# Quantising three late weight matrices inside feed-forward instead of in setup

## The chip, the cores and the metric

The kernel runs on one core of one Trainium2 chip. The metric is the device time of one execution in microseconds (us); less is better. A core has five engines with their own instruction streams, which wait for each other by semaphores: TensorE (PE, matmuls and transposes into the eight PSUM banks; PEld is its weight load), VectorE (DVE), ScalarE (ACT), GpSimd (POOL) and SyncE (SP), which here issues every DMA. All DMAs stand in SyncE's stream in a fixed order.

## The reference

x is (4, 512, 512): 2048 tokens of width 512. Four residual steps follow one another:

```python
x = x + jnp.tanh(g_xattn[0]) * _L0_xattn_ref(4, 512, 512, L0_xattn_w, L0_xattn_u, _layernorm(x, axis=-1), ctx_2048)
x = x + jnp.tanh(g_ffn[0]) * _L0_ffn_ref(_layernorm(x, axis=-1), L0_ffn_w1, L0_ffn_w2, L0_ffn_w3)
x = x + jnp.tanh(g_xattn[1]) * _L1_xattn_ref(_layernorm(x, axis=-1), ctx_2048, L1_xattn_wq, L1_xattn_bq, L1_xattn_wkv, L1_xattn_bkv, L1_xattn_wp, L1_xattn_bp)
x = x + jnp.tanh(g_ffn[1]) * _L1_ffn_ref(_layernorm(x, axis=-1), L1_ffn_gamma, L1_ffn_W)
```

The first is a decayed running ratio along the sequence ("mixing"), the second a gated feed-forward with sign weights and group-quantised activations, the third 16-head attention, the fourth a quantised linear layer ("output"). Three 512x512 matrices are quantised before use. wq and wp get one scale per output row, absolute maximum over 127, and integers `clip(round(x / s), -127, 127)`. W of the output layer (`wl` in the kernel) gets one scale for all of it: `clip(round(W * w_scale), -1, 1)` with `w_scale = 1 / (mean|W| + 1e-5)`. Keys and values are `cond @ wkv.T + bkv`, and wkv (1024x512) is not quantised.

## The kernel before

Everything is held in SBUF. X holds the 2048 tokens as 16 row tiles of 128. The stages follow one another.

**Setup** (lines 334 to 348 and the opening part of each engine). Small vectors, three rows spread over all partitions (bv_all, bp_all, gam_all), wkv, X, the first context, wq, wp and wl are loaded. wkv is split into a high f16 part (ScalarE, L665) and a low one (VectorE, L1324). Fourteen groups of eight TensorE transposes (L974, T_GROUPS) turn wkv's two parts (groups 0 to 7), wq, wp and wl (8 to 13); ScalarE copies the even groups out of PSUM (L674), VectorE the odd ones (L1336). Ahead of groups 8 to 13 VectorE finds the maxima of wq and wp (L1341, L1342), rounds (L1347) and makes integers (L1349), and does the same for wl with the mean of its absolute values (L1353 to L1358), which ScalarE has summed (L671) and TensorE spread (L980). wp's scales are spread over the partitions by a diagonal matrix (L1362, L982, L676, swp_all). VectorE also takes the statistics of all 16 X tiles (L1328, L1367), GpSimd the deviations (L500, L501). All engines go on to mixing when the last copies are out.

**Mixing** (16 steps s; b is the batch, k one of four blocks of 128 features). GpSimd normalises x four blocks ahead (`normed`, L519) and forms the numerators (L510). TensorE turns the keys and the context (`context_turn`, L1006, `key_turn`) and projects keys (L1034) and values (L1045). ScalarE makes exponentials, signs of a piece of w1, w2, w3 (L745), and the logarithm and exponential that give the inverse (L706, L708). VectorE runs two scans (L1443, L1454) and the ratio of the step before (`ratio`, L1396), adds bv_all to the values (`values`, L1408) and adds to X (L1383). SyncE stores keys and values, loads pieces and turns the signs by DMA (`turn_weights`, L366).

**Feed-forward** (16 row tiles i, each in four quarters j; c = 4i + j numbers the quarters). TensorE runs `up(i, j)`, 16 matmuls with W1T and W2T, and then `down(i-1, j)`, 8 with W3T. W1's matmuls of quarter c wait for `d_done` of quarter c-2. ScalarE runs `silu`, `round_up` (L780) and `high` (L785), VectorE `hidden` (L1509 to L1514) and `scaled` (L1520), GpSimd the low part (L563), and SyncE turns both parts by one DMA per quarter (`turn_h`, L413) and x of the next tile (`turn_x`, L387). Between the quarters VectorE, ScalarE and GpSimd prepare x for tile i+2 (`prep_...`) and attention's queries (`q_...`, from tile 2 on). Tiles 2k and 2k+1 are one call `tiles(k)`; k = 0, 1 and 7 are written out, 2 to 6 are a loop.

Attention and output follow. WQT is first read at tile 4 (`q_project(0)`, L1100), WPT and WLT in the output stage. Nothing plans the order: each engine does what its own code says, in that order.

## Time and profile before

| | us |
|---|---|
| median of three runs | 973.86 (973.63 to 978.19) |
| the profiled execution | 978.03 |
| its span, first to last instruction | 976.3 |
| TensorE busy | 826.5 (85%) |
| VectorE busy | 760.4 (78%) |
| ScalarE busy | 573.4 (59%) |
| GpSimd busy | 484.2 (50%) |

Setup lasts until about 55 us, mixing until about 220, feed-forward until about 585. Times in a timeline count from the first instruction. "[0.77 <-DVE B L1520]" behind a row says that the engine sat idle for 0.77 us before it, and that VectorE's instruction of line 1520 ended the wait. Durations in the working are of the profiled execution, and sums are made against its 978.03.

### The profile page before, as it was taken

The numbers are of one execution on the slowest core, as the hardware profiler recorded it, in microseconds if no ns is written. First come the engines' busy times: TensorE is split into PE (matmuls) and PEld (weight loads), VectorE is DVE, ScalarE is ACT, GpSimd is POOL, SyncE is SP. The second block draws the span as 40 slices with busy tenths as digits, with TensorE's granted clock in tenths as the row PEclk, the third lists the DMA queues.
The fourth block names the chain that finished last, engine by engine and source line by source line (L and its number), as shares of the span: only waits on it lengthen the run. The fifth ranks groups of instructions, "written<-read, shape, count | busy, mean of one in ns | idle before, by whom it ended". The sixth has DMA issues, their size and how long they took to land.

```text
span 976.3 us, 15239 instructions
## 1 busy us (share of the span) xinstructions
PE 826.5 (85%) x4423; PEld 359.1 (37%) x4423; DVE 760.4 (78%) x1505; ACT 573.4 (59%) x965; POOL 484.2 (50%) x560
## 2 busy tenths in 40 slices
PE   1379988778999999999999978799999999974654
PEld 1235444333444444444444433132323232222321
DVE  3958998887899998999999758477777777724884
ACT  2347888753455656556566554466666666665762
POOL 1086556322334444434444343476767666664761
PEclk9559999989999999999999995799999999996885
DMA  8536987652233323232323332312222121000111
GB/s 278 217 101 181 216 231 194 157 151 45 56 64 64 67 56 62 54 64 54 64 54 61 60 84 69 85 56 62 71 61 70 52 78 49 1 1 0 44 64 65
DMA packets 165163, 84.51 MB, mean 87 GB/s; under 512 B 116960, under 2 KB 149872, under 8 KB 165104
## 3 DMA queue, kind: packets, MB, share of 16 engines
q1 hardware_dynamic: 165104, 83.81, 34.1%
q8 instruction: 27, 0.44, 0.2%
q14 instruction: 32, 0.26, 0.1%
HBM read 37.50 MB, written 12.58 MB: 51 GB/s over the span
## 4 chain that ended last, share of the span: by engine, by line
PE 55%; DVE 8%; SPq 4%; issue 4%; ACT 3%; DMA 3%; POOL 0%; ACTq 0%; DVEq 0%
PE bank L1070 21%; PE bank L1082 10%; PE bank L1157 5%; PE bank L1128 5%; PE bank L1147 4%; DMA A<-B 3%; SPq L432 2%; PE bank L1273 2%; PE bank L1176 2%; PE bank L1166 2%; PE bank L1100 1%; SPq L441 1%; DVE X L1730 1%; DVE B L1611 1%; PE bank L1136 1%
## 5 line engine op out<-in xcount | busy, mean ns | idle before, releaser
L1070 PE MATMUL bank<-A,B 128*128 128x512 f16 x1024 | 232.4, 380 | 3.9 <-DVE B L1520 3.9
L1603 DVE TENSOR_REDUCE B<-bank 128x1 f32<-128x512 f32 x256 | 168.1, 683 | 73.4 <-PE bank L1128 73.3
L895 ACT ACTIVATE A<-bank 128x512 f32<-128x512 f32 x256 | 144.1, 593 | 107.0 <-PE bank L1147 103.5
L563 POOL TENSOR_TENSOR B<-B 128x512 f16<-128x512 f32 x64 | 75.5, 1180 | 209.1 <-ACT B L785 154.7
L1070 PEld LDWEIGHTS bank<-A,B 128*128 128x128 f16 x1024 | 100.2, 98 | 126.2 <-DVE B L1520 4.6
L637 POOL TENSOR_TENSOR B<-A 128x512 f32<-128x512 f32 x64 | 79.4, 1270 | 94.4 <-ACT A L895 94.4
L1082 PE MATMUL bank<-A,B 128*128 128x512 f16 x512 | 120.7, 379 | 0.0
L780 ACT ACTIVATE bank<-B 128x512 f32<-128x512 f32 x64 | 38.5, 602 | 124.6 <-DVE B L1514 124.4
L1147 PE MATMUL bank<-A 98*128 98x512 f16 x256 | 94.9, 392 | 19.5 <-ACT A L895 10.9
L1128 PE MATMUL bank<-A 96*128 96x512 f16 x256 | 98.0, 410 | 7.6 <-DMA A<-B 4.2
L637 POOL TENSOR_TENSOR B<-B,A 128x512 f32<-128x512 f32 x64 | 79.1, 1265 | 1.7 <-ACT A L895 1.7
L1157 PE MATMUL bank<-A,B 128*32 128x512 f32 x512 | 70.4, 623 | 1.0 <-ACT A L895 1.0
L1082 PEld LDWEIGHTS bank<-A,B 128*128 128x128 f16 x512 | 49.5, 98 | 54.3 <-DMA B<-B 0.4
L1045 PE MATMUL bank<-B 128*128 128x512 f16 x192 | 48.4, 406 | 16.7 <-DVE B L1408 16.6
L1520 DVE SCALAR_TENSOR_TENSOR B<-bank,gsm 128x512 f32<-128x512 f32 x64 | 44.2, 691 | 17.1 <-ACT bank L780 15.7
L1509 DVE SCALAR_TENSOR_TENSOR bank<-bank,ffs,B 128x512 f32<-128x512 f32 x64 | 48.3, 755 | 9.4 <-PE bank L1070 6.3
L1128 PEld LDWEIGHTS bank<-A 96*128 96x128 f16 x256 | 23.3, 100 | 84.5 <-DVE B L1603 65.3
L519 POOL TENSOR_SCALAR B<-X,mv,rs 128x128 f32<-128x128 f32 x64 | 49.8, 792 | 1.2 <-DVE WLT L1336 1.2
L775 ACT ACTIVATE B<-bank,ffs 128x512 f32<-128x512 f32 x64 | 43.0, 671 | 10.8 <-PE bank L1070 10.4
L1147 PEld LDWEIGHTS bank<-A 98*128 98x128 f16 x256 | 25.1, 99 | 65.8 <-ACT A L895 36.9
L785 ACT CAST B<-B 128x512 f16<-128x512 f32 x64 | 39.5, 618 | 11.3 <-DVE B L1520 11.3
L1034 PE MATMUL bank<-B 128*128 128x512 f16 x192 | 46.0, 391 | 0.0
(231 smaller groups left out, 1484.1 us busy)
## 6 DMA issues: line engine op xcount, KB each, us to landing
B<-in_L_ffn_w_dram SPq DMA_DIRECT2D x48, 256.0 KB, 3.8
A<-k_parts SPq DMA_DIRECT2D x48, 128.0 KB, 2.6
A<-B SPq DMA_DIRECT2D x192, 32.0 KB, 1.9
X<-in_x_dram SPq DMA_DIRECT2D x4, 1024.0 KB, 13.6
B<-in_ctx_dram SPq DMA_DIRECT2D x16, 256.0 KB, 5.2
k_parts<-B SPq DMA_DIRECT2D x16, 256.0 KB, 4.5
...
```

The costliest lines, as they stand in the source:

```text
L519: last_ = nc.gpsimd.tensor_scalar(XN[:, t, cols], X[:, i, cols], mv[:, i:i + 1, 0], rs[:, i:i + 1], ALU.subtract, ALU.mult)
L563: nc.gpsimd.tensor_tensor(HLb[j][:, 1, :], Db[j % 2], HLb[j][:, 0, :], ALU.subtract).then_inc(lo_done, 1)
L637: nc.gpsimd.tensor_tensor(ACC[j], PR[j] if t == 1 else ACC[j], PR[(HG * t + j) % 8], ALU.add).then_inc(acc_done, 1)
L895: nc.scalar.activation(PR[(HG * t + j) % 8], bank[2 + j % 2][:, :], ACT.Exp, scale=SCALE).then_inc(exp_done, 1)
L1045: last_ = mm(bank[7][:, :], cx[:, j, k * P:k * P + P], wt[:, j, D:2 * D], start=(p == 0 and j == 0), stop=(p == 2 and j == DB - 1))
L1070: last = mm(bank[2 * n + q][:, :], XQT[a][:, m, :], wt[:, m % DB, j * 512:j * 512 + 512], start=(m == 0), stop=(m == 2 * DB - 1))
L1082: last = mm(bank[5 + q][:, :], HT[j][:, m, :], W3T[:, DB * j + m % DB, :], start=(j == 0 and m == 0), stop=(j == FC - 1 and m == 2 * DB - 1))
L1128: mm(bank[ROW_BANKS[r % 3]][:, :], QS[0:96, HG * g + j, t * P:t * P + P], KS[0:96, HG * g + j, :], start=True, stop=True).then_inc(row_ps, 1)
L1147: mm(bank[2 + j % 2][:, :], KS[0:98, HG * g + j, t * P:t * P + P], QS[0:98, HG * g + j, :], start=True, stop=True).then_inc(st_ps, 1)
L1157: last_ = mm(bank[6][DH * j:DH * j + DH, :], VB[:, t, (HG * g + j) * DH:(HG * g + j + 1) * DH], PR[(HG * t + j) % 8], start=(t == 0), stop ...
L1509: stt(H, H, C2, SAb[q], ALU.mult, ALU.mult).then_inc(h_done, 1)
L1603: reduce(NMX[g % 2][:, t, j:j + 1], bank[ROW_BANKS[r % 3]][:, :], AX.X, ALU.max, negate=True).then_inc(row_max, 1)
```

## The change

Setup keeps only wkv. It is loaded in two halves (keys' rows, values' rows) with the first quarter of X between them, and turned half by half, in eight groups. The three spread rows are loaded after the first pieces, behind X's second quarter, and `values(0)` waits for them (`wide_in`). The statistics of X's later batches stand in mixing: those of batch 1 before step 0, one tile of batch 2 or 3 at the start of each step from 0 to 7. GpSimd's deviations stand at steps 0, 4 and 8.

wq, wl and wp go through one buffer (wm_raw, wm_ints) in this order, one to each pair of tiles m = 0, 1, 2:
- SyncE loads wq when mixing is over. At tile 2 it turns the integers of wq by four DMAs into WQT and loads wl; at tile 4 it turns those of wl and loads wp; at tile 6 it turns those of wp, writes wp's scales to memory, waits, and loads them spread into swp_all.
- VectorE: `matrix_scale(m)` (maxima) ahead of quarter 2 of tiles 0 and 4, `mean_scale` ahead of quarter 2 of tile 2, `matrix_ints(m)` ahead of quarter 1 of tiles 1, 3 and 5.
- ScalarE: `matrix_round(m)` at quarter 3 of tiles 0, 2 and 4, `matrix_sum` (sum of |wl|) at quarter 1 of tile 2.
- TensorE: the one-column matmul of that sum at tile 2 behind `up` of quarter 2. The loop now has four turns, and `tiles(2)` is written out.

The core of the diff (eight leading spaces taken off each line):

```diff
+T_GROUPS = [(raw, turned, g) for h in range(2) for raw, turned in ((wkv_hi, WKVH), (wkv_lo, WKVL))
+            for g in (2 * h, 2 * h + 1)]
+WKV_HALF = [slice(4 * D * h, 4 * D * h + 4 * D) for h in range(2)]
...
                     (vrows[12:16, :], by_block(bkv[0:D])),
-                    (TG[:, 0:2], on_all(g_xattn, 2)), (TG[:, 2:4], on_all(g_ffn, 2)),
-                    (bv_all[:, :], on_all(bkv[D:2 * D], D)), (bp_all[:, :], on_all(bp, D)),
-                    (gam_all[:, :], on_all(gamma, D))):
+                    (TG[:, 0:2], on_all(g_xattn, 2)), (TG[:, 2:4], on_all(g_ffn, 2))):
         sp.dma_start(to, frm).then_inc(small_in, 16)
-    sp.dma_start(wkv_raw.rearrange("p (k d) -> p k d", d=D), tiled(wkv)).then_inc(wkv_in, 16)
-    sp.dma_start(X[:, 0:TB, :], x_rows[:, 0:TB, :]).then_inc(x_in[0], 16)
+    for h in range(2):
+        sp.dma_start(wkv_raw[:, WKV_HALF[h]].rearrange("p (k d) -> p k d", d=D),
+                     tiled(wkv)[:, 4 * h:4 * h + 4, :]).then_inc(wkv_in[h], 16)
+        if h == 0:
+            sp.dma_start(X[:, 0:TB, :], x_rows[:, 0:TB, :]).then_inc(x_in[0], 16)
...
-    sp.dma_start(wq_raw, tiled(wq)).then_inc(wqp_in, 16)
-    sp.dma_start(wp_raw, tiled(wp)).then_inc(wqp_in, 16)
-    sp.dma_start(wl_raw, tiled(wl)).then_inc(wl_in, 16)
-    for b in range(1, BATCH):
-        sp.dma_start(X[:, TB * b:TB * b + TB, :], x_rows[:, TB * b:TB * b + TB, :]).then_inc(x_in[b], 16)
...
     pieces(0)
+    sp.dma_start(X[:, TB:2 * TB, :], x_rows[:, TB:2 * TB, :]).then_inc(x_in[1], 16)
+    for to, frm in ((bv_all[:, :], on_all(bkv[D:2 * D], D)), (bp_all[:, :], on_all(bp, D)),
+                    (gam_all[:, :], on_all(gamma, D))):
+        sp.dma_start(to, frm).then_inc(wide_in, 16)
+    for b in range(2, BATCH):
+        sp.dma_start(X[:, TB * b:TB * b + TB, :], x_rows[:, TB * b:TB * b + TB, :]).then_inc(x_in[b], 16)
     for n in range(DB, 2 * DB):
         next_context(n)
...
+    def load_matrix(m):
+
+        if m == 0:
+            sp.wait_ge(mixed, DB * BATCH)
+            sp.wait_ge(key_lo, DB * BATCH)
+        else:
+            sp.wait_ge(wm_ready, m)
+        sp.dma_start(wm_raw, tiled((wq, wl, wp)[m])).then_inc(wm_in, 16)
+
+    def turn_matrix(m):
+
+        sp.wait_ge(wm_ready, m + 1)
+        for k in range(DB):
+            sp.dma_start_transpose((WQT, WLT, WPT)[m][:, :, k * P:k * P + P], wm_ints[:, k, :]).then_inc(wm_out, 16)
+
+    def spread_scale():
+
+        sp.dma_start(swp_dram.rearrange("(k p) -> p k", p=P), SWQP[:, 4:8],
+                     allow_slow_non_contiguous=True).then_inc(swp_io, 16)
+        sp.wait_ge(swp_io, 16)
+        sp.dma_start(swp_all[:, :], on_all(swp_dram, D)).then_inc(swp_io, 16)
+
+    load_matrix(0)
     sp.wait_ge(ff_scales, 1)
     for i in range(TOK):
+        if i in (2, 4, 6):
+            turn_matrix(i // 2 - 1)
+        if i in (2, 4):
+            load_matrix(i // 2)
+        if i == 6:
+            spread_scale()
...
     nc.gpsimd.memset(held[:, :], 0.0).then_inc(consts_set, 1)
-    for b in range(BATCH):
+    def deviations(b):
         cols = slice(TB * b, TB * b + TB)
         pool.wait_ge(stats_ready, b + 1)
...
         nc.gpsimd.tensor_tensor(PHL[:, 1, :], PD, PHL[:, 0, :], ALU.subtract).then_inc(xlo, 1)
-    pool.wait_ge(small_out_dve, 7)
-    pool.wait_ge(small_out_act, 7)
+    deviations(0)
...
     numerators(0)
     for s in range(DB * BATCH):
         k = s % DB
+        if k == 0 and s + DB < DB * BATCH:
...
     step = Chain(act, act_step)
-    act.wait_ge(wkv_in, 16)
...
-    act.wait_ge(wl_in, 16)
-    nc.scalar.activation(T32[:, 2:6, :], wl_raw, ACT.Abs, accum_out=PART[:, 3:4]).then_inc(wl_sum, 1)
-    for g in range(0, len(T_GROUPS), 2):
-        act.wait_ge(small_turned, g + 1)
-        nc.scalar.copy(turned_rows(g), bank_rows(g)).then_inc(small_out_act, 1)
-    act.wait_ge(setup_ps, SETUP["swp_ps"])
-    nc.scalar.copy(swp_all[:, :], bank[7][:, :]).then_inc(small_out_act, 1)
+    for h in range(2):
+        act.wait_ge(wkv_in[h], 16)
+        nc.scalar.activation(wkv_hi[:, WKV_HALF[h]], wkv_raw[:, WKV_HALF[h]], ACT.Copy,
+                             scale=WUP).then_inc(wkv_hi_done, 1)
+        if h == 1:
+            for g in range(0, len(T_GROUPS), 2):
+                act.wait_ge(small_turned, g + 1)
+                nc.scalar.copy(turned_rows(g), bank_rows(g)).then_inc(small_out_act, 1)
...
         up_to(act, hT_in[j], i * 16)
         nc.scalar.copy(HLb[j][:, 0, :], Db[j % 2]).then_inc(hi_done, 1)
+    def matrix_round(m):
+
+        act.wait_ge(wm_scale, m + 1)
+        if m == 1:
+            nc.scalar.activation(wm_raw, wm_raw, ACT.Copy, bias=RND, scale=WS).then_inc(wm_round, 1)
+        else:
+            c = 0 if m == 0 else 4
+            for k in range(DB):
+                last_ = nc.scalar.activation(wm_raw[:, k, :], wm_raw[:, k, :], ACT.Copy, bias=RND,
+                                             scale=RWQP[:, c + k:c + k + 1])
+            last_.then_inc(wm_round, 1)
+
+    def matrix_sum():
+
+        act.wait_ge(wm_in, 16 * 2)
+        nc.scalar.activation(QALL[:, 0, :, 0:2 * 512].bitcast(F32), wm_raw, ACT.Abs,
+                             accum_out=PART[:, 3:4]).then_inc(wm_round, 1)
+
     def q_norm(u):
         act.wait_ge(rstd3, u + 1)
             more = not (last and a == 1)
             for j in range(FC):
                 c = FC * i + j
+                if isinstance(k, int) and k == 1 and (a, j) == (0, 1):
+                    matrix_sum()
...
+                if isinstance(k, int) and k == 1 and (a, j) == (0, 2):
+                    pe.wait_ge(wm_round, SUMMED)
+                    mm(bank[7][:, 0:1], ones[:, :], PART[:, 3:4], start=True, stop=True).then_inc(setup_ps, 1)
                 if not (first and a == 0):
                     down(i - 1, j, 1 - a)
...
+    for h in range(2):
+        dve.wait_ge(wkv_hi_done, h + 1)
+        stt(wkv_lo[:, WKV_HALF[h]], wkv_raw[:, WKV_HALF[h]], WUP, wkv_hi[:, WKV_HALF[h]],
+            ALU.mult, ALU.subtract).then_inc(wkv_lo_done, 1)
+
+    def batch_stats(b, t):
         dve.wait_ge(x_in[b], 16)
-        for t in range(TB):
-            last = nc.vector.bn_stats(st[:, TB * b + t, :], X[:, TB * b + t, :])
-        link(last)
-        for t in range(TB):
-            last = nc.vector.bn_aggr(mv[:, TB * b + t, :], st[:, TB * b + t, :])
-        last.then_inc(stats_ready, 1)
-
-    def small_out(g):
+        i = TB * b + t
+        link(nc.vector.bn_stats(st[:, i, :], X[:, i, :]))
+        last = nc.vector.bn_aggr(mv[:, i, :], st[:, i, :])
+        if t == TB - 1:
+            last.then_inc(stats_ready, 1)
+
+    for t in range(TB):
+        batch_stats(0, t)
...
-        for t in range(TB):
-            last = nc.vector.bn_aggr(mv[:, TB * b + t, :], st[:, TB * b + t, :])
-        last.then_inc(stats_ready, 1)
-    small_out(9)
-    small_out(11)
...
+        if s == 0:
+            dve.wait_ge(wide_in, 16 * 3)
...
+    for t in range(TB):
+        batch_stats(1, t)
     for s in range(DB * BATCH):
         k = s % DB
+        if s + 2 * DB < DB * BATCH:
+            batch_stats(s // DB + 2, k)
         if s > 0:
             ratio(s - 1)
...
+    def matrix_scale(m):
+
+        dve.wait_ge(wm_in, 16 * (m + 1))
+        c = 0 if m == 0 else 4
+        link(reduce(ABSM[:, c:c + 4], wm_raw, AX.X, ALU.max, apply_absolute_value=True))
+        link(ts(SWQP[:, c:c + 4], ABSM[:, c:c + 4], 1.0 / 127.0, 1e-8, ALU.mult, ALU.max))
+        recip(RWQP[:, c:c + 4], SWQP[:, c:c + 4]).then_inc(wm_scale, 1)
+
+    def mean_scale():
+
+        dve.wait_ge(setup_ps, SETUP["wl_mean_ps"])
+        link(ts(LSC, bank[7][:, 0:1], 1.0 / (D * D), 1e-5, ALU.mult, ALU.add))
+        recip(WS, LSC).then_inc(wm_scale, 1)
+
+    def matrix_ints(m):
+
+        dve.wait_ge(wm_round, ROUNDED[m])
+        up_to(dve, wm_out, 16 * DB * m)
+        if m != 1:
+            ts(wm_ints, wm_raw, RND, 127.0, ALU.subtract, ALU.min).then_inc(wm_ready, 1)
+        else:
+            link(ts(wm_raw, wm_raw, RND, -1.0, ALU.subtract, ALU.max))
+            ts(wm_ints, wm_raw, 1.0, None, ALU.min).then_inc(wm_ready, 1)
+
     def tiles(k, first, last):
         for a in range(2):
             i = 2 * k + a
             for j in range(FC):
                 c = FC * i + j
+                if isinstance(k, int) and k < 3 and (a, j) == (0, 2):
+                    mean_scale() if k == 1 else matrix_scale(k)
+                if isinstance(k, int) and k < 3 and (a, j) == (1, 1):
+                    matrix_ints(k)
                 hidden(c, j % 2)
```

Where it moves instructions. A row is an instruction of the named line with its tiles, its shape and what it waits for; x4 stands for four alike. B and A are the two large buffers.

VectorE behind wkv's low part, before:

```order
L1336 COPY B<-bank 128x4x256 [waits small_turned] x2
L1341 TENSOR_REDUCE vec<-A 128x4 [waits wqp_in]
L1342 TENSOR_REDUCE vec<-A 128x4
L1343 TENSOR_SCALAR vec<-vec 128x8 [waits dve_step]
L1344 RECIPROCAL vec<-vec 128x8 [waits dve_step]
L1347 TENSOR_SCALAR A<-A,vec 128x512 [waits dve_step]
L1347 TENSOR_SCALAR A<-A,vec 128x512 x3
L1349 TENSOR_SCALAR B<-A 128x2048 [waits dve_step]
```

and now (L1387 is the copy of the turned groups, L1391 what came last in setup, L1405 mixing's first `low_context`):

```order
L1378 BN_STATS st<-X 128x6 [waits x_in0]
L1379 BN_AGGR mv<-st 128x2 [waits dve_step]
L1387 COPY B<-bank 128x4x256 [waits small_turned] x4
L1391 TENSOR_SCALAR ffs<-vec 128x1 [waits vec_act,consts_set,small_out_act]
L1405 TENSOR_TENSOR B<-bank,B 128x512 [waits ctx_vt,ctx_hi,dve_step]
L1405 TENSOR_TENSOR B<-bank,B 128x512 [waits ctx_vt,ctx_hi] x3
L1378 BN_STATS st<-X 128x6 [waits x_in1]
```

The maxima, roundings and integers are gone from between the copies, and the statistics stand ahead of all four copies and again ahead of mixing's first scan.

SyncE at tiles 1 and 2 of feed-forward (`turn_h` is L413 before and L412 now, `turn_x` L387 and L380), before:

```order
L413 DMA_TRANSPOSE B<-B 128x8x128 [waits down_ps,lo_done,hi_done]
L387 DMA_TRANSPOSE B<-B 128x8x128 [waits b_ps,xlo,xhi]
L413 DMA_TRANSPOSE B<-B 128x8x128 [waits down_ps,lo_done,hi_done] x4
L387 DMA_TRANSPOSE B<-B 128x8x128 [waits b_ps,xlo,xhi]
L413 DMA_TRANSPOSE B<-B 128x8x128 [waits down_ps,lo_done,hi_done] x4
```

and now:

```order
L412 DMA_TRANSPOSE B<-B 128x8x128 [waits down_ps,lo_done,hi_done]
L380 DMA_TRANSPOSE B<-B 128x8x128 [waits b_ps,xlo,xhi]
L412 DMA_TRANSPOSE B<-B 128x8x128 [waits down_ps,lo_done,hi_done] x3
L455 DMA_TRANSPOSE WQT<-B 128x4x128 [waits wm_ready]
L455 DMA_TRANSPOSE WQT<-B 128x4x128 x3
L449 DMA B<-in_L_ffn_W_dram 128x4x512 [waits wm_ready]
L412 DMA_TRANSPOSE B<-B 128x8x128 [waits down_ps,lo_done,hi_done]
L380 DMA_TRANSPOSE B<-B 128x8x128 [waits b_ps,xlo,xhi]
L412 DMA_TRANSPOSE B<-B 128x8x128 [waits down_ps,lo_done,hi_done] x4
```

Four transposes to WQT and wl's load stand between tile 1's last `turn_h` and tile 2's first.

ScalarE at tile 2 (`high` of quarter 0, then `prep_hi`, `round_up`, `silu` and `high` of quarter 1), before:

```order
L785 CAST B<-B 128x512 [waits hT_in0,d_done]
L731 CAST B<-B 128x512 [waits xhl,xT_in0]
L780 ACTIVATE bank<-B 128x512 [waits silu_done,t_done]
L775 ACTIVATE B<-bank,ffs 128x512 [waits h_done,a_ps]
L785 CAST B<-B 128x512 [waits hT_in1,d_done]
```

and now (L831 is `matrix_sum`):

```order
L814 CAST B<-B 128x512 [waits hT_in0,d_done]
L831 ACTIVATE B,ffs<-B 128x4x512 [waits wm_in]
L760 CAST B<-B 128x512 [waits xhl,xT_in0]
L809 ACTIVATE bank<-B 128x512 [waits silu_done,t_done]
L804 ACTIVATE B<-bank,ffs 128x512 [waits h_done,a_ps]
L814 CAST B<-B 128x512 [waits hT_in1,d_done]
```

The sum over wl, which waits for its load, has come between `high` of quarter 0 and all of quarter 1.

## Rows read from the trace of the kernel before

**Rows 1.** Busy table, 12 us: span, PE, PEld, DVE, ACT, POOL, granted clock, DMA, GB/s.

```profile
36.00:48.00 12.00, 3.42 (x33) 2.86 (x32) 11.79 (x25) 3.04 (x3) 1.20 (x2) 0.60 0.19 68
```

**Rows 2.** Timeline of VectorE in setup: start, duration, line, tiles, shapes, [idle before, releaser].

```profile
18.23 4.42 DVE L1324 SCALAR_TENSOR_TENSOR A<-A 128x4096 f16<-128x4096 f32 x1 [6.22 <-ACT A L665]
...
26.54 2.27 DVE L1341 TENSOR_REDUCE vec<-A 128x4 f32<-128x2048 f32 x1
...
33.20 1.23 DVE L1349 TENSOR_SCALAR B<-A 128x2048 f16<-128x2048 f32 x1
...
53.40 0.69 DVE L1336 COPY WLT<-bank 128x1024 f16<-128x1024 f16 x1 [0.53 <-PE bank L974]
```

**Rows 3.** Timeline of TensorE in setup.

```profile
18.25 3.40 PE L974 MATMUL bank<-id,A 128*128 128x128 f16 x32 [8.77 <-ACT A L665]
...
55.85 1.09 PE L1006 MATMUL bank<-id,B 128*128 128x128 f32 x8 [0.68 <-ACT swp_all L676]
```

**Rows 4.** Timeline of GpSimd at the end of setup.

```profile
54.36 12.43 POOL L519 TENSOR_SCALAR B<-X,mv,rs 128x128 f32<-128x128 f32 x16 [1.22 <-DVE WLT L1336]
66.75 1.27 POOL L510 TENSOR_TENSOR B<-B 128x512 f32<-128x512 f32 x1
```

**Rows 5.** Timeline of VectorE in mixing's steps 0 and 1.

```profile
65.34 1.23 DVE L1443 TENSOR_TENSOR_SCAN bank<-vec,bank 128x512 f32<-128x512 f32 x1 [2.73 <-ACT bank L699]
...
72.25 0.70 DVE L1396 TENSOR_TENSOR bank<-bank,B 128x512 f32<-128x512 f32 x1 [2.46 <-ACT B L708]
```

**Rows 6.** Waits from 60 to 228: who waits, for whom, us in total, times, longest.

```profile
DVE bank L1396 <- ACT B L708: 8.2, 8, 2.5
```

**Rows 7.** Timeline of TensorE in feed-forward.

```profile
239.32 3.61 PE L1070 MATMUL bank<-A,B 128*128 128x512 f16 x16 [0.77 <-DVE B L1520]
...
286.63 3.62 PE L1070 MATMUL bank<-A,B 128*128 128x512 f16 x16
...
346.90 3.40 PE L1070 MATMUL bank<-A,B 128*128 128x512 f16 x15
```

**Rows 8.** Timeline of VectorE in feed-forward.

```profile
285.25 0.69 DVE L1520 SCALAR_TENSOR_TENSOR B<-bank,gsm 128x512 f32<-128x512 f32 x1
...
344.49 0.69 DVE L1520 SCALAR_TENSOR_TENSOR B<-bank,gsm 128x512 f32<-128x512 f32 x1 [0.67 <-ACT bank L780]
```

**Rows 9.** DMA issues: out<-in, times issued, KB each, median us to landing.

```profile
out_dram<-X SPq DMA_DIRECT2D x8, 512.0 KB, 2.8
A<-in_L_xattn_wkv_dram SPq DMA_DIRECT2D x1, 2048.0 KB, 10.0
...
A<-B SPq DMA_TRANSPOSE x48, 2.5
```

**Rows 10.** Timeline of ScalarE in setup.

```profile
14.58 3.62 ACT L665 ACTIVATE A<-A 128x4096 f16<-128x4096 f32 x1 [12.49 <-DMA A<-in_L_xattn_wkv_dram]
```

**Rows 11.** Timeline of VectorE in feed-forward, statistics of one tile.

```profile
229.39 0.69 DVE L1415 BATCH_NORM_STATS2 st<-X 128x6 f32<-128x512 f32 x1
...
230.12 0.18 DVE L1417 BATCH_NORM_AGGREGATE mv<-st 128x2 f32<-128x6 f32 x1
```

**Rows 12.** Timeline of ScalarE in feed-forward's tiles 0 to 2.

```profile
243.80 0.60 ACT L780 ACTIVATE bank<-B 128x512 f32<-128x512 f32 x1 [3.97 <-DVE B L1514]
...
269.80 0.62 ACT L785 CAST B<-B 128x512 f16<-128x512 f32 x1 [0.15 <-DVE B L1520]
...
273.84 0.60 ACT L780 ACTIVATE bank<-B 128x512 f32<-128x512 f32 x1 [2.91 <-DVE B L1514]
```

**Rows 13.** Timelines of SyncE's queue, and of GpSimd in tile 1.

```profile
212.83 3.84 SPq L366 DMA_TRANSPOSE A<-B  x3
...
265.84 1.16 POOL L563 TENSOR_TENSOR B<-B 128x512 f16<-128x512 f32 x1 [4.78 <-ACT B L785]
```

**Rows 14.** Timeline of TensorE in mixing's last steps.

```profile
193.02 5.30 PE L1045 MATMUL bank<-B 128*128 128x512 f16 x12 [3.64 <-DVE B L1408]
```

**Rows 15.** Busy table, 2 us; columns as in rows 1, clock third from the end.

```profile
194.00:196.00 2.00, 2.00 (x7) 0.62 (x6) 1.49 (x2) 1.52 (x3) 1.15 (x1) 0.50 0.65 174
```

More of the change, by code:

```diff
@@ L843, in _ @@
             tiles(1, False)
-            with act.Fori(2, TOK // 2 - 1) as k:
+            tiles(2, False)
+            with act.Fori(3, TOK // 2 - 1) as k:
                 tiles(k, False)
@@ L1117, in _ @@
             tiles(1, False, False)
-            with pe.Fori(2, TOK // 2 - 1) as k:
+            tiles(2, False, False)
+            with pe.Fori(3, TOK // 2 - 1) as k:
                 tiles(k, False, False)
@@ L1374, in _ @@
[L1374 to L1375 removed]
+            dve.wait_ge(small_out_act, len(T_GROUPS) // 2)
+            dve.wait_ge(consts_set, CONSTS["all"])
             dve.wait_ge(vec_act, 2)
```

122 lines of the change are left out of this document (40 added, 82 removed).

## The prediction

> **What bounds the kernel now.** I read four views in this order: the busy table by stretches, the timelines of the engines through setup, the waits and the timeline of mixing's steps, and the timelines of feed-forward's first tiles. In setup TensorE has next to nothing to do: 3.42 us of the 12 us from 36 on, while VectorE is busy for 11.79 [rows 1]. VectorE is working through the three later matrices, and it hands over the last copy of WLT at 53.4 to 54.1 [rows 2]. Only then do TensorE's context transposes start, at 55.85 [rows 3], and GpSimd's sixteen normalising instructions, at 54.36; these take 12.43 and the numerators behind them end at 68.02 [rows 4]. The weights and scans of step 0 come at 65.34, and the first ratio waits 2.46 for ScalarE's logarithm and starts at 72.25 [rows 5]. In mixing VectorE is nearly full: over 16 steps its ratio waits 8.2 us in all, eight times, 2.5 of it in step 1 [rows 6]. In feed-forward's tile 0 TensorE waits for VectorE (0.77 before the group at 239.32), and after that it never stops [rows 7]. But VectorE is only just ahead. The W1 matmuls of quarter c need VectorE's scaled quarter c-2: that of quarter 13 is done at 285.25 + 0.69 = 285.94 and the matmuls start at 286.63, a lead of 0.69; for quarter 24 it is 344.49 + 0.69 = 345.18 against 346.90, a lead of 1.72 [rows 7, 8]. So work that is put on VectorE there is paid for in full, but for about 1.4 us once.
>
> **Setup: what goes.** Time before is counted against the profiled execution. The path is now: second half of wkv, its high part, VectorE's low part, VectorE's statistics, its four copies, contexts.
> - wkv's 2 MB landed about 10.0 us after issue [rows 9], and ScalarE started on it at 14.58 [rows 10]. The new order puts wkv half, X, wkv half: 3 MB, but without the three broadcast loads ahead of them (0.75 MB), so the second half should land at much the same time. At wkv's 5.0 us per MB X adds 5.0 and the broadcasts drop 3.8, which gives 15.8; but part of X was in flight while wkv landed, so I take 14.7. Bounds 13.5 (all of X was) and 17.7 (the broadcasts had cost only half of that).
> - Half of the 3.62 high part [rows 10] is 1.8: 16.5. Half of the 4.42 low part [rows 2] is 2.2: 18.7. Four linked pairs of statistics at 0.69 + 0.18, overlapping to about 0.84 a pair [rows 11], are 3.4: 22.1.
> - The copies now stand behind the statistics. First two 1.3 (0.69 each [rows 2]); TensorE turns group 5 after the first, then 6 and 7, at 3.40/4 = 0.85 each [rows 3]: 22.8 + 2.6 = 25.4; last copy 0.7: 26.1.
> The contexts start at 26.1 where they started at 55.85: **29.7 earlier**. GpSimd no longer waits for the copies: it needs the statistics (22.1), 1.3 for the deviation, then 12.43 and 1.27 [rows 4], so the numerators are there at 37.2, 30.8 earlier. VectorE puts four more statistics pairs (3.4) and one of step 0 (0.8) in front of the first scan. They shift it from 65.34 - 29.7 + 1.5 to about 37.4, but step 1's ratio waited 2.46 anyway [rows 5], so the first ratio comes 29.4 earlier. I take **-29.4**; bounds -31 (wkv at 13.5) and -26 (at 17.7).
>
> **Mixing: what comes in.** Eight statistics pairs stand ahead of the ratio in steps 0 to 7, 0.84 each. That of step 0 and that of step 1 lie in the waits just named. Six are left: 5.0. The other seven waits of the ratio hold 5.7 in all [rows 6]; I count 3 of it, the half that falls into these steps and the one after, as filled by the new work. **+2**; bounds 0 and +5. The three GpSimd deviation pairs (1.2 each) stand before work that GpSimd does early, at nothing; if that cover were gone they would cost 1.2 three times. In values(0) the wait for the wide rows is free: they land some 20 us before.
>
> **Feed-forward: what comes in.** I follow VectorE's delay D and TensorE's delay, which is D less the lead.
> - Tile 0, quarter 2: absolute maximum of wq, 2.27 [rows 2], and two small instructions, 2.76 with links. TensorE already waits for VectorE here: D = 2.8. ScalarE's four roundings in quarter 3 take about 2.6 and fit into its wait of 3.97 [rows 12].
> - Tile 1, quarter 1: integers of wq, 1.23 [rows 2]: D = 4.0.
> - Tile 2 is the dear one. SyncE gets to WQT's transposes when it has issued those of quarter 7; GpSimd's low part of it ended at 265.84 + 1.16 = 267.0 [rows 13], now 271.0. Then 1.2 for that transpose, four of 1.28 (3.84 for three [rows 13]), so the load of wl is issued at about 277.4 and 1 MB lands some 4.5 later (512 KB took 2.8 [rows 9]), at 282. ScalarE is at its abs-sum after the cast of quarter 8, which ended at 270.4 [rows 12], now 274.4, and stands **7.6 us** with everything behind it: its own sum of 1.91 (half of the 3.62 for 4096 columns, [rows 10]), prep_hi's 0.6, and the rounding of quarter 9. This rounding started at 273.84 [rows 12], would be at 277.8, and is at 284.6: 6.8 later, D = 10.8. TensorE waits for the same sum before the down-projection. Bounds 5.5 (load lands in 3.2) and 9.
> - Quarter 10: two small ones, 0.4. Tile 3, quarter 1: WLT's clamp and integers, twice 1.23: D = 13.7.
> - Tile 4: the same queue for wp. The load lands about 1 us after VectorE asks; with 2.76 for the maximum D = 17.5. ScalarE's roundings again fit. Tile 5: 1.23, D = 18.8.
> - TensorE's delay is 18.8 - 1.4 = **17.4**.
> - Tile 6: SyncE issues four transposes (5.1), writes 512 single words, waits until they have landed and issues the broadcast. The transpose of tile 7's x stands behind. It needs to land some 15 us after quarter 23 and does so after about 1.2 + 5.1 + 4.5 + 0.5 + 1.3 + 2.5 [rows 9] = 15.1. No row shows such a write: it can't take less than nothing, and by its 512 pieces I set it at 4.5, above the 2.8 of [rows 9]; with the h transpose that also stands ahead I count **+1.2**, bounds 0 and +5.
> - **+0.9** for the clock, below. Feed-forward: **+19.5**, bounds +13 and +26.
>
> **The clock.** Before the twelve value matmuls at 193.02 TensorE stood idle for 3.64 and they took 5.30 [rows 14], at a granted clock of 0.50, which is 1.2 GHz [rows 15]; at 2.4 GHz they would take half. The wait in tile 2 is longer, the one in tile 4 about as long. So 2 to 3 us of matmuls run at 1.2 GHz after each. After tile 2 VectorE's 2.5 us of tile 3 cover it; after tile 4 about 0.9 sticks. The Trainium skill (TensorE: Matmul & The Clock Gate, "HAM oscillation") says that every wait that re-throttles the array is paid again in slow matmuls; by that rule alone both would cost, some 2.5 each, and the total would be 4 us higher than mine. The trace agrees on the halved clock; whether it is hidden behind VectorE no row shows.
>
> **Sum**: -29.4 + 2 + 19.5 = -7.9. The profiled execution took 978.03 and would take 970.1; the median of the three runs is 973.86, so the forecast is **966.0**. Attention and the output stage are the same instructions on the same data.
>
> **The rivals.**
> 1. *Feed-forward costs its work alone.* If wl and wp land before they are asked for, the 6.8 shrinks to sum and prep_hi that fit into the wait of 2.91 [rows 12], and the 1 us of tile 4 and the clock's share go: about 9 less, 957. For it: the loads are only 1 MB. Against: SyncE can't issue them before four transposes. Chance 0.17.
> 2. *Both ends are dearer.* The second wkv half lands at 17.7 (+3) and mixing swallows none of the pairs (+3), or both waits drag the clock: 970 to 978, say 974. For it: VectorE is the fullest engine in mixing. Chance 0.23.
> 3. *Slower: the matrices' transposes go one after the other.* If each holds the queue for its own 2.5 us [rows 9] rather than for 1.28 of issue, each matrix takes 10 instead of 5. Then the waits of tiles 2 and 4 are 5 longer each and tile 7's x lands 5 later: 966 + 15 = 981. It decides from the point where one transpose holds the queue over 2.3 us. Against: three issued in 3.84 let ScalarE go on soon after. The Trainium skill (Advanced Engine Details and Errata, X-Bar Transpose) calls them as fast as plain transfers on this chip; no row here sets the two side by side. Chance 0.12.
> 4. *It doesn't take setup off the path*, because something else still holds the contexts until about 55: none of the engines has such work left. Chance 0.03: about 990.
>
> **How the numbers follow.** Forecast 0.45 (960 to 971), and the rivals as given. A measurement tells about 0.5%, 4.9 us, from no change: faster is below 969.0, slower above 978.7. Faster: 0.17, and three quarters of 0.45, and a little of rival 2: 0.54. Slower: 0.12 + 0.03 and the top of rival 2: 0.16. Same: 0.30. Range 955 to 978: it leaves out rivals 3 and 4.
>
> **What would show it.** First context transpose near 26, first ratio near 43, feed-forward's first matmul near 193 (220.64 - 27.4). ScalarE's abs-sum should show a wait of 7 to 8 for a DMA, TensorE one of about 6 before the single-column matmul, and the feed-forward stage should be 19 longer. A stage only 10 longer is rival 1; contexts after 30 or ratios that no longer wait at all are rival 2; waits of over 12 in tile 2 are rival 3.

## The result, and the profile after

The changed kernel takes **978.88 us** (median of 20 runs), the kernel before beside it 976.64 (20 runs): ratio 1.003, 95% interval 1.0021 to 1.0039. Forecast were 966.0, with 955 to 978. So 29 us of setup were won, and feed-forward spent slightly more than that. The profiled execution has a span of 975.0 at a mean granted clock of 0.948. It is the shortest of its 20 (976.90), and that of the kernel before (978.03) lies 1.4 above its median. So the two traces compared below differ by -1.1 where the medians differ by +2.2; these 3.4 us are not explained here.

Setup of the changed kernel, as timelines give it (start, duration, engine, line, tiles, shapes, count, [idle before, releaser]). The first three rows answer [rows 3] and [rows 4], the last answers [rows 5].

```profile
26.31 1.09 PE L1045 MATMUL bank<-id,B 128*128 128x128 f32 x4 [0.83 <-ACT B L705]
...
23.55 12.43 POOL L546 TENSOR_SCALAR B<-X,mv,rs 128x128 f32<-128x128 f32 x16
35.94 1.27 POOL L537 TENSOR_TENSOR B<-B 128x512 f32<-128x512 f32 x1
...
43.15 0.70 DVE L1410 TENSOR_TENSOR bank<-bank,B 128x512 f32<-128x512 f32 x1 [0.48 <-ACT B L737]
```

Contexts at 26.31 instead of 55.85, the first ratio at 43.15 instead of 72.25: 29.1 earlier.

Where it went is read at one landmark per quarter: the start of VectorE's first instruction on a quarter's hidden rows (line 1509 before, 1529 after), in both timelines. Each tile has four. The fourth column is how much of the gain the tile spent.

| tile | quarter 0, before | after minus before | spent in the tile | forecast |
|---|---|---|---|---|
| 0 | 225.39 | -29.20 | 2.3 | 2.8 |
| 1 | 245.27 | -26.88 | 1.0 | 1.2 |
| 2 | 265.69 | -25.85 | 8.4 | 7.2 |
| 3 | 286.87 | -17.48 | 3.5 | 2.5 |
| 4 | 308.47 | -13.99 | 5.0 | 3.8, and 0.9 of clock |
| 5 | 330.36 | -9.00 | 1.0 | 1.3 |
| 6 | 352.59 | -8.01 | 7.2 | 1.2 |
| 7 | 374.48 | -0.81 | 0.2 | 0 |
| 8 to 13 | 396.74 | -0.59 | 0.1 | 0 |
| 14 | 528.98 | -0.52 | 1.5 | 0 |
| 15 | 549.58 | +1.00 | 0 | 0, and 1.4 of lead given back |

Feed-forward spent 30.2 where 19.5 were forecast (1.4 of lead taken off), and mixing nothing where 2 were. Behind the landmark of tile 15 the difference goes from +1.0 to -1.3 at the end of the span. That is attention and the output stage, the same instructions on both sides; over all the runs below this part comes out between -2.3 and +0.7, and nothing here says why.

The landmark is VectorE's. TensorE's groups of 16 matmuls tell the end of the story better:

```profile
349.18 3.62 PE L1109 MATMUL bank<-A,B 128*128 128x512 f16 x16
...
376.09 3.62 PE L1109 MATMUL bank<-A,B 128*128 128x512 f16 x16
...
546.92 3.62 PE L1109 MATMUL bank<-A,B 128*128 128x512 f16 x16
```

Before, these three groups start at 358.15, 375.09 and 545.92. So TensorE is 8.97 early in the middle of tile 6, and from the second quarter of tile 7 on it is 1.00 late. From there to tile 15 it never waits, in either trace, and the 1.00 stays. By TensorE's reckoning the stretch around tile 6 costs 10.0 and not 7.2, and tile 14 costs nothing: the 1.5 there is only VectorE's distance from TensorE that changes.

The dear tiles, in the timelines of ScalarE, VectorE and TensorE:

```profile
253.69 1.91 ACT L831 ACTIVATE B<-B 128x2048 f32<-128x2048 f32 x1 [9.13 <-DMA B<-in_L_ffn_W_dram]
...
255.75 0.59 PE L1157 MATMUL bank<-ffs,ones 128*128 128x1 f32 x2 [7.55 <-ACT B L831]
256.20 3.20 PE L1121 MATMUL bank<-A,B 128*128 128x512 f16 x8
...
307.79 2.29 DVE L1580 TENSOR_REDUCE vec<-B 128x4 f32<-128x2048 f32 x1 [2.66 <-DMA B<-in_L_xattn_wp_dram]
...
368.55 5.08 PE L1109 MATMUL bank<-A,B 128*128 128x512 f16 x16 [8.35 <-DMA B<-B]
```

In tile 2 ScalarE stands 9.13 at the sum of absolute values, and TensorE 7.55 for that sum. In tile 4 VectorE waits 2.66 for the third matrix. At the start of tile 7 TensorE waits 8.35 for a DMA, x's transpose; the kernel before has no such stop. SyncE's queue shows what stood ahead of these DMAs: the first two rows are of tile 2, the others of tile 6.

```profile
242.49 5.20 SPq L455 DMA_TRANSPOSE WQT<-B  x4
247.74 0.58 SPq L449 DMA_DIRECT2D B<-in_L_ffn_W_dram  x1
...
346.74 5.20 SPq L455 DMA_TRANSPOSE WPT<-B  x4
351.98 0.58 SPq L459 DMA_DIRECT2D swp_row<-vec  x1
360.80 0.33 SPq L462 DMA_DIRECT2D swp_all<-swp_row  x1
361.24 3.63 SPq L412 DMA_TRANSPOSE B<-B  x1
364.98 1.25 SPq L380 DMA_TRANSPOSE B<-B  x1
```

The load of the second matrix is issued at 247.74, behind four transposes. The write of the 512 scales is issued at 351.98, and only at 360.80, 8.8 later, can SyncE go on. It issues the broadcast of the scales, then the transpose of hidden rows, whose issue takes 3.63 where 1.23 is usual; x's transpose (line 380) follows at 364.98.

### The profile page after: what moved, and what is told of

The parts are those of the page before. It is cut to its first block, busy times and chain, and to the rows that moved or that the text cites. A ratio compares the mean times of both kernels' runs of the same rounds, so it can differ in the third digit from the quotient of the medians.

```text
span 975.0 us, 15020 instructions
## 1 busy us (share of the span) xinstructions
PE 822.8 (84%) x4373; PEld 354.8 (36%) x4373; DVE 750.3 (77%) x1492; ACT 576.2 (59%) x971; POOL 487.7 (50%) x560
## 4 chain that ended last, share of the span: by engine, by line
PE 43%; DVE 15%; issue 6%; SPq 6%; DMA 5%; ACT 4%; POOL 1%; ACTq 0%; DVEq 0%; POOLq 0%
PE bank L1109 13%; PE bank L1121 6%; PE bank L1203 5%; PE bank L1174 5%; PE bank L1193 4%; DMA A<-B 3%; PE bank L1320 2%; SPq L431 2%; PE bank L1222 2%; PE bank L1212 2%; DVE bank L1529 2%; SPq L455 2%; DVE gsm L1531 1%; DVE B L1534 1%; DVE B L1540 1%
## 5 line engine op out<-in xcount | busy, mean ns | idle before, releaser
L1109 PE MATMUL bank<-A,B 128*128 128x512 f16 x1024 | 236.0, 384 | 19.7 <-DVE B L1540 11.3
L1121 PE MATMUL bank<-A,B 128*128 128x512 f16 x512 | 121.9, 382 | 0.0
L1193 PE MATMUL bank<-A 98*128 98x512 f16 x256 | 93.8, 388 | 20.6 <-ACT A L947 10.9
L1529 DVE SCALAR_TENSOR_TENSOR bank<-bank,ffs,B 128x512 f32<-128x512 f32 x64 | 48.4, 757 | 22.3 <-PE bank L1109 20.2
L1531 DVE TENSOR_REDUCE gsm<-bank 128x8 f32<-128x512 f32 x64 | 44.3, 692 | 2.2
```

Source lines behind the costliest of these rows:

```text
L1109: last = mm(bank[2 * n + q][:, :], XQT[a][:, m, :], wt[:, m % DB, j * 512:j * 512 + 512], start=(m == 0), stop=(m == 2 * DB - 1))
L1121: last = mm(bank[5 + q][:, :], HT[j][:, m, :], W3T[:, DB * j + m % DB, :], start=(j == 0 and m == 0), stop=(j == FC - 1 and m == 2 * DB - 1))
L1193: mm(bank[2 + j % 2][:, :], KS[0:98, HG * g + j, t * P:t * P + P], QS[0:98, HG * g + j, :], start=True, stop=True).then_inc(st_ps, 1)
L1529: stt(H, H, C2, SAb[q], ALU.mult, ALU.mult).then_inc(h_done, 1)
L1531: link(reduce(gsm[:, 0, :], grouped(H), AX.X, ALU.max, apply_absolute_value=True))
```

## The experiments

Each landmark difference below is, as above, against the kernel before, in the profiled execution. Each ratio is against runs of the kernel before on the same chip.

**Setup alone.** Edit: every call of `load_matrix`, `turn_matrix`, `spread_scale`, `matrix_scale`, `mean_scale`, `matrix_round`, `matrix_sum` and `matrix_ints` out, and a constant in their tiles, set by GpSimd ahead of tile 0. The kernel then leaves out the quantising, and its output is not the reference's.

```diff
-                if i in (2, 4, 6):
-                    turn_matrix(i // 2 - 1)
-                if i in (2, 4):
-                    load_matrix(i // 2)
-                if i == 6:
-                    spread_scale()
```

> Left out: all of the three matrices' work in feed-forward (loads, sums, maxima, rounding, integers, the twelve transposes, the scattered write and its broadcast); the tiles that later read them hold a constant instead, so the output is not the reference's. My theory: setup gives its 29 us and mixing keeps them, and everything that was lost was lost in feed-forward. Quarter 0 of tile 0 then stands 29.2 us before that of the kernel before, and the last quarter of tile 15 too: 976.6 - 29.3 = 947 us, between 945 and 950. Rival A: feed-forward of the changed kernel loses time also without the matrices' work (the batches' statistics, the wide rows, a clock that falls): over 955. Rival B: attention gives some of the lead back: feed-forward ends 29 earlier, but the time is over 952.

Measured: 946.17, ratio 0.9694 (0.967 to 0.9718). The landmark is at -29.68 in tile 0, -29.69 in tile 3, -30.58 in tile 8 and -29.68 in tile 15. Setup's gain is whole, mixing and attention take nothing of it, and all that the changed kernel lost is the matrices' work in feed-forward.

**The wait for the scattered write moved to tile 8** (write_apart), and **the loads issued early** (load_early), alone and together (both_moves).

```diff
             def spread_scale():
...
-                sp.wait_ge(swp_io, 16)
-                sp.dma_start(swp_all[:, :], on_all(swp_dram, D)).then_inc(swp_io, 16)
+            def fetch_scale():
+                sp.wait_ge(swp_io, 16)
+                sp.dma_start(swp_all[:, :], on_all(swp_dram, D)).then_inc(swp_io, 16)
...
+                if i == 8:
+                    fetch_scale()
```

```diff
-                if i in (2, 4):
-                    load_matrix(i // 2)
...
                 for j in range(FC):
+                    if i in (1, 3) and j == 2:
+                        load_matrix((i + 1) // 2)
                     turn_h(i, j)
```

> All is computed. The scattered write of the 512 scales is issued at tile 6 as before, but SyncE waits for it and issues the broadcast at tile 8. My theory: the wait for that write (351.98 to 360.80 in the changed kernel) held the transposes of tile 6 and with them tile 7's x; of the 7.2 us that tile 6 costs, 5.5 to 7.2 go: 971.7 to 973.5 us, and no wait of TensorE over 2 us near the start of tile 7. Rival A: the four matrix transposes ahead of it (5.2 us of SyncE) are what held x, and the write came beside: at most 3 us go, 976 us or more, with a wait of 4 us or more left at tile 7. Rival B: the wait at tile 8 only moves the loss there: 978 to 980 us.

> All is computed. The loads of the second and the third matrix are issued ahead of the third quarter's transpose of tiles 1 and 3 (as soon as the buffer is free) and no longer behind the four transposes of tiles 2 and 4, so they land over 15 us earlier. My theory: ScalarE's 9.13 us wait at the sum of absolute values and the 2.7 us wait ahead of the third matrix's maximum go. Tile 2 then costs 2 to 4 us and not 8.4, tile 4 2.8 to 3.5 and not 5.1: together 6 to 8.5 us less, 970.5 to 973 us. Rival A: the cost is the passes themselves, which VectorE and ScalarE execute at whatever time: 977 us or more. Rival B: the earlier loads now hold the transposes of tiles 1 and 3 (a transpose behind a load took 2.29 to 2.85 us to issue, not 1.23), and give back 2 to 3 us: 974 to 976 us.

> All is computed. Both edits of write_apart and load_early. My theory: the waits are at different tiles and the lead of VectorE does not carry from one to the other, so the gains add up: 963.5 to 967.5 us, which is 9 to 13 us faster than the kernel before. Rival A: one of the two waits covered part of the other's cost (while TensorE stands, VectorE catches up and pays for passes that otherwise cost time themselves), so that 3 us or more of the sum is missing: 968 to 971 us.

Measured: 975.8, ratio 0.9997 (0.9982 to 1.0011); 966.93, 0.9904 (0.9877 to 0.993); 963.16, 0.9867 (0.9843 to 0.9892). load_early saved more than expected, 10.9 us at tile 15's landmark: tile 2 now spends nothing (landmark -26.57 to -26.87, a gain of 0.3) instead of 8.4, and tile 4 2.3 instead of 5.0. ScalarE's sum starts without a wait; the load had been issued at 231.54.

```profile
243.75 1.91 ACT L831 ACTIVATE B<-B 128x2048 f32<-128x2048 f32 x1
```

So ScalarE's whole pass is free there; what tiles 0, 3 and 4 still spend (2.3, 3.5 and 2.3) is near the length of VectorE's passes, and for these alone rival A holds. write_apart missed: tile 6 still spends 4.4 of its 7.2, or 6.5 of 10.0 by TensorE. Its SyncE queue and TensorE:

```profile
352.76 0.58 SPq L459 DMA_DIRECT2D swp_row<-vec  x1
353.45 1.24 SPq L412 DMA_TRANSPOSE B<-B  x1
354.80 1.27 SPq L380 DMA_TRANSPOSE B<-B  x1
...
365.56 6.10 PE L1114 MATMUL bank<-A,B 128*128 128x512 f16 x16 [3.80 <-DMA B<-B]
```

x's transpose is issued at 354.80 and not at 364.98, but TensorE gets x only 10.8 later. SyncE's wait was only part of the matter. both_moves adds the gains up. The ratios fell from 1.003 to 0.9997 and 0.9904 by the single edits and to 0.9867 by both, which is 1.6 points either way; at tile 15's landmark it is 14.8 against 10.9 and 2.0, where single profiles of one setup already differ by 1 us at tile 0's.

**The write behind x** (write_after_x, on top of both_moves).

```diff
-                if i == 6:
-                    spread_scale()
                 for j in range(FC):
                     turn_h(i, j)
                     if j == 0 and i < TOK - 1:
                         turn_x(i + 1, (i + 1) % 2)
+                    if i == 6 and j == 0:
+                        spread_scale()
```

> All is computed. both_moves, with the scattered write of the scales issued in tile 6 behind the transpose of tile 7's x and no longer ahead of it. In both_moves and write_apart x was issued in time (354.80) and still landed at 365.6, while the 16 DMA engines were busy and moved 8 to 33 GB/s. My new theory: the write itself keeps the DMA engines for 8 to 10 us and what is issued behind it lands behind it; behind x it only delays hidden rows, which are due a tile later. Tile 6 then costs under 0.7 and not 4.2 us: 958.5 to 960 us. Rival A: the four matrix transposes ahead of x are what delays it: 962.5 us or more, with TensorE's wait of 3 us or more left. Rival B: the delayed transposes of hidden rows hold TensorE's second multiplication: 960 to 963 us, with waits on those rows.

Measured: 955.42, ratio 0.9787 (0.9762 to 0.9813); once more, with five rounds, 954.43, ratio 0.9776 (0.9748 to 0.9803).

> The kernel of write_after_x once more, beside sliced_two_turns on the same chip, to tell the two apart and to set its gain on the kernel before: 955 to 957 us, ratio 0.977 to 0.981.

```profile
334.15 5.21 SPq L455 DMA_TRANSPOSE WPT<-B  x4
339.46 1.24 SPq L412 DMA_TRANSPOSE B<-B  x1
340.81 1.27 SPq L380 DMA_TRANSPOSE B<-B  x1
342.14 0.57 SPq L459 DMA_DIRECT2D swp_row<-vec  x1
...
347.46 3.62 PE L1114 MATMUL bank<-A,B 128*128 128x512 f16 x16
```

The four matrix transposes still stand ahead of x, and TensorE starts tile 7 at 347.46 without a wait; tile 6 spends nothing (-20.59 to -21.14; TensorE stays at -21.56). The four transposes thus cost nothing, and the order of two DMAs is worth some 8 us.

**Queue or engines** (write_on_act, write_on_act_late): the write is issued by ScalarE, on a queue of its own; in the first between tiles 5 and 6, in the second inside tile 6, which is written out for it.

```diff
             tiles(2, False)
+            act.dma_start(swp_dram.rearrange("(k p) -> p k", p=P), SWQP[:, 4:8],
+                          allow_slow_non_contiguous=True).then_inc(swp_io, 16)
```

```diff
+                        if isinstance(k, int) and k == 3 and (a, j) == (0, 1):
+                            act.dma_start(swp_dram.rearrange("(k p) -> p k", p=P), SWQP[:, 4:8],
+                                          allow_slow_non_contiguous=True).then_inc(swp_io, 16)
                         if more and j == 1:
                             x_turned(act, k, a)
                             prep_hi(i + 1)
```

> All is computed. both_moves, with the scattered write issued by ScalarE, on a DMA queue of its own, between tiles 5 and 6; SyncE's queue has only its transposes there. If the order in SyncE's queue is what delays x, the wait of 3.8 us goes: 958.5 to 960.5 us. If the 512 small elements keep the DMA engines themselves, whichever queue they are in, x lands as late as in both_moves: 962 to 964 us. I hold the engines for likelier, 6 to 4.

> All is computed. In write_on_act the write was issued at 330.3, so that it had landed (9.5 us) when tile 7's x was issued at 340.68, and that run does not tell the queue from the engines. Here ScalarE issues it in tile 6, right ahead of its last operation on x, 1 to 3 us before SyncE issues x's transpose (in both_moves SyncE's own queue had the write 2 us ahead of x, and TensorE went on 12.3 us after the write, having waited 4.04). If what waits is only what stands behind the write in the same queue: no wait of TensorE for x, 954 to 957 us. If the 512 small elements keep the DMA engines for everyone: x lands some 12 us after the write's issue, a wait of 3 to 5 us as in both_moves, 960 to 963 us. I now hold the queue for likelier, 6 to 4: in the changed kernel the DMA engines stood at a busy share of 0.44, 0.10, 0.00 and 0.00 in the four stretches of 2 us in which SyncE waited for the write.

Measured: 956.68, ratio 0.9796 (0.9776 to 0.9816), and 957.91, ratio 0.9801 (0.9779 to 0.9824). For x the first can't tell the two apart: it issued the write at 330.3, and its landing 9.5 later was over before x was issued. But SyncE's transposes right behind it tell:

```profile
330.31 0.41 ACTq L895 DMA_DIRECT2D swp_row<-vec  x1
...
332.27 1.23 SPq L412 DMA_TRANSPOSE B<-B  x1
```

This one landed 9.3 after its issue, where 3.0 is the median of the kernel before, and the four matrix transposes behind it 8.3 down to 5.2, where write_after_x has 2.5. They came late although the write was in another queue, and it cost nothing, since none of them was due. The second run shows the same for x:

```profile
337.06 0.40 ACTq L877 DMA_DIRECT2D swp_row<-vec  x1
...
341.66 1.27 SPq L380 DMA_TRANSPOSE B<-B  x1
...
350.70 5.31 PE L1112 MATMUL bank<-A,B 128*128 128x512 f16 x16 [2.24 <-DMA B<-B]
```

Nothing but transposes is in SyncE's queue, and TensorE still waits 2.24 and goes on 9.0 after x's issue and 13.6 after the write's; in both_moves it was 12.3 after the write's. So in both profiled executions a queue of its own did not protect what SyncE issued behind the write, and my 6 to 4 for the queue was the wrong way. How much it helps is open: the second's execution was the longest of five, 962.4 with a median of 957.9, which lies between the two forecasts, so in others x may have waited less. Busy table of the same run (span, PE, PEld, DVE, ACT, POOL, clock, DMA share, GB/s):

```profile
342.00:344.00 2.00, 2.00 (x11) 0.90 (x10) 1.94 (x7) 1.85 (x4) 0.35 (x1) 1.00 2.12 70
344.00:346.00 2.00, 2.00 (x11) 0.94 (x10) 1.86 (x5) 0.23 (x1) 1.77 (x5) 1.00 1.57 13
```

The 16 engines have packets open for all of the time and move 13 GB/s in the second stretch. When the write was alone in the changed kernel, the share was 0.10 and 0.00 from 354 to 358, so it is slow without filling the engines. Whether it is the elements in DRAM or their acknowledgement that takes 9 us, no run tells.

**The second matrix's passes where GpSimd is idle** (ints_quiet, on top of write_after_x).

```diff
-                        if isinstance(k, int) and k < 3 and (a, j) == (1, 1):
+                        if isinstance(k, int) and k in (0, 2) and (a, j) == (1, 1):
                             matrix_ints(k)
                         hidden(c, j % 2)
+                        if isinstance(k, int) and k == 1 and (a, j) == (1, 3):
+                            matrix_ints(k)
```

> All is computed. write_after_x, with the second matrix's two passes on VectorE moved from the start of the second quarter of tile 3 to the inside of its fourth, and what follows for the third matrix one or two quarters later. In the changed kernel these passes took 2.18 and 2.06 us, and GpSimd's subtractions beside them 2.13, while in setup the same passes took 1.23 and GpSimd's 1.15. My theory: the two engines' 128-partition passes hinder each other when they meet; in the fourth quarter GpSimd is idle by then, so the passes take 1.2 to 1.3 us each, and 1.5 to 2.1 us less than write_after_x are seen at tile 3; the time is 1 to 2 us under write_after_x's. Rival: the passes are slower for another reason that holds all through feed-forward (the transfers, the place of the buffer): 2.0 us or more each, and no difference.

Measured: 955.75, ratio 0.9774 (0.975 to 0.9798), not told apart from write_after_x. But the passes did as expected. First the changed kernel, at tile 3 with GpSimd beside them and at tile 1 with VectorE's start just ahead of GpSimd's, then ints_quiet:

```profile
274.52 2.18 DVE L1597 TENSOR_SCALAR B<-B 128x2048 f32<-128x2048 f32 x1
275.58 2.13 POOL L560 TENSOR_TENSOR B<-B 128x512 f16<-128x512 f32 x1
276.74 2.06 DVE L1598 TENSOR_SCALAR B<-B 128x2048 f16<-128x2048 f32 x1
...
223.30 1.20 DVE L1595 TENSOR_SCALAR B<-B 128x2048 f16<-128x2048 f32 x1
223.33 2.17 POOL L591 TENSOR_TENSOR B<-B 128x512 f16<-128x512 f32 x1 [3.14 <-DVE B L1540]
```

```profile
279.44 1.22 DVE L1602 TENSOR_SCALAR B<-B 128x2048 f32<-128x2048 f32 x1
280.69 1.23 DVE L1603 TENSOR_SCALAR B<-B 128x2048 f16<-128x2048 f32 x1
```

From tile 2's third quarter to tile 4's second the landmark loses 1.8 and not 3.3 as in write_after_x; the third matrix's work, which had to move too, then costs 0.6 more (its integers 2.0 and not 1.4). So it is shown that the two engines hinder each other here; the 0.9 that is left is too little for the measurement. The rows say more than that. In the changed kernel the later starter pays: at tile 1 VectorE began 0.03 ahead of GpSimd and took its 1.20, and GpSimd took 2.17 instead of 1.16. At tile 3 GpSimd had begun 0.27 ahead (line 591, 274.25 to 275.62), and VectorE's first pass took 2.18; the subtraction that began inside that pass took 2.13.

**Work in slices** (sliced, sliced_two_turns). All of the matrices' work is cut in blocks of 128 x 512, with three load buffers; one block in a quarter. The core of VectorE's part, with c the quarter counted from tile 0, and the edit that makes sliced_two_turns of sliced, which had one such transpose for each c from 12 to 15 (the mean of the second matrix also comes a quarter earlier, at c = 14):

```diff
+                            if 2 <= c < 6:
+                                matrix_max(0, c - 2)
+                            if 8 <= c < 12:
+                                matrix_ints(0, c - 8)
+                            if 12 <= c < 16:
+                                matrix_max(2, c - 12)
...
+                    if c in (12, 13):
+                        turn_matrix(0, 2 * j)
+                        turn_matrix(0, 2 * j + 1)
```

> All is computed. The matrices are loaded into three buffers of their own, at tiles 0, 1 and 2, and all of their work is cut in blocks of 128 x 512: one block in a quarter of a tile on ScalarE and VectorE (on VectorE between the scaling and the rounded result, where it waits for ScalarE), one transpose in a quarter on SyncE, the scattered write behind the second quarter of tile 6. In the kernel before VectorE is idle for some 39 of 360 us in feed-forward, 0.6 us in a quarter. My theory: passes of 0.3 to 0.9 us in a quarter mostly fit in there, and only what is over 0.6 costs: 2 to 5 us over setup_alone's 946.2, 948 to 951.5 us. Rival A: what is executed on VectorE costs in full however it is cut, since its lead is used up by the next quarter: some 12 to 14 us, 958 to 961 us. Rival B: the finer work adds waits and instructions: 953 to 957 us.

> All is computed. sliced, with the first matrix's four transposes two in each of tile 3's first two quarters (they were one in each of its four), and the mean of the second matrix a quarter earlier. In sliced, TensorE waited 9.2 us ahead of the first projection of queries: it is due at the start of tile 4, and the last transpose was issued only at 285.09, behind the hidden rows of tile 3's last quarter. My theory: that wait goes whole (7.5 us at the landmark of tile 4), and the blocks cost 6 to 8 us over setup_alone's 946.2: 952 to 954.5 us, 1 to 3.5 under write_after_x. Rival: the 9.2 us gave VectorE and ScalarE time for blocks that they now pay for elsewhere: 955 to 958 us, no faster than write_after_x.

Measured: 960.02, ratio 0.9825 (0.9806 to 0.9845), and 952.23, ratio **0.9746 (0.9719 to 0.9773)**. sliced was slow by a wait that I had built in. Its last transpose of WQT stood behind tile 3's last hidden rows:

```profile
285.09 1.27 SPq L458 DMA_TRANSPOSE WQT<-B  x1
...
287.82 1.87 PE L1146 MATMUL bank<-B,WQT 128*128 128x128 f16 x16 [9.19 <-issue]
```

With two transposes in each of two quarters this wait is gone and so are the 7.5 us at the landmark. The fixed version spends 6.5 from tile 0 to tile 6 (-30.88 to -24.36), write_after_x 9.8. What is sliced does not vanish in VectorE's idle time, as I had hoped (rival A was nearer for sliced, but for another reason), but about 3 us less are spent; the three load buffers and other partners on GpSimd came with it, and how much each of them gave was not separated. It is 24.7 us faster than the kernel before and the fastest that does all of the work; beside write_after_x on the same chip it is 2.2 us faster, at overlapping intervals.

## Why the prediction was wrong

- **Tile 6, +1.2: the step that failed.** It priced the scattered write's landing at 4.5, above a plain transfer's 2.8, and that nearest row was far off: it took 8.8. My bound "0 and +5" was also made for one of its effects only, that SyncE stands still. The other is that what is issued behind the write lands late, from whichever queue. TensorE waited 8.35 for x, and the 16 matmuls behind took 5.08 instead of 3.62. Together TensorE lost 10.0, of which 7.2 show at VectorE's landmark. With the write behind x the stretch costs nothing. This step alone is 8.8 of the 10.7 that feed-forward cost more than forecast; all that stands ahead of it cost TensorE 20.2 where 18.3 were forecast.
- **Setup, -29.4**: right, -29.1 at the first ratio. The path of contexts (forecast 26.1, measured 26.31) and of numerators (37.2 and 37.21) held row by row.
- **Mixing, +2**: too dear. The landmark at tile 0 is -29.2 here and -29.7 in setup_alone. All eight statistics pairs found cover, not only half.
- **Tile 0 and tile 1**: 2.3 and 1.0 for 2.8 and 1.2, right; VectorE's passes are paid for in full there, as [rows 7, 8] suggested.
- **Tile 2, 7.2** (6.8 and the 0.4 of quarter 10): 8.4. The mechanism was right to the place: the load was issued at 247.74 where 248.0 had been worked out, and load_early shows that the wait was the whole price. The term was short in the landing (5.93 after issue, not 4.5). Rival 1's statement, that sum and rounding cost nothing if the load is there, is what load_early measured.
- **Tile 3, 2.5**: 3.5, since the two passes of 1.23 took 2.18 and 2.06 beside GpSimd. Tile 4, 3.8: 5.0, a wait of 2.66 for "about 1".
- **The lead of 1.4** came back in part: in tile 6 TensorE is 8.97 early and VectorE 8.00, so 1.0 of it was there before the wait for x.
- **The clock, +0.9**: slow matmuls came, but not where they were priced.

```profile
282.84 5.27 PE L1109 MATMUL bank<-A,B 128*128 128x512 f16 x16 [2.22 <-DVE B L1540]
...
314.64 3.61 PE L1109 MATMUL bank<-A,B 128*128 128x512 f16 x16 [2.70 <-DVE B L1540]
```

  At tile 4, where the 0.9 was put, 16 matmuls took 3.61 behind a wait of 2.70, at a granted clock of 1.00: nothing was lost. In tile 2 eight took 3.20 instead of 1.89, and in tile 3 sixteen took 5.27 instead of 3.62, at a clock of 0.50 (1.2 GHz). Both were covered, as had been said of tile 2: from 256 to 290 no instruction waits for TensorE, and tile 3 spends the same 3.5 in load_early, where its sixteen took 3.63. At tile 7, where nothing had been put, they were paid in full. The wait and what the sixteen took over 3.62 add up to 9.8, 6.3, 6.5 and 3.9 in the changed kernel, write_apart, both_moves and write_on_act_late, and TensorE lost 10.0, 6.5, 6.6 and 4.1. The Trainium skill (TensorE: Matmul & The Clock Gate, "HAM oscillation") has every such wait paid again in slow matmuls; the trace agrees at tile 7 (1.46) and not at tiles 2 and 3.
- **The base**: the sum was set on a median of three runs, 973.86. From the 976.64 of 20 runs it gives 968.7, so 2.8 of the 12.9 us by which 966.0 was off are not the working's.
- **Rival 3** had the nearest time (981) by the wrong cause: the matrices' transposes are issued in 1.3 each and cost nothing in write_after_x, where all twelve still run.
